# A second wait ahead of GpSimd's row gathers in a one-core graph-attention, mixing and expert kernel

## The reference

```python
xn = _layernorm(x)
h  = xn @ W_layer.T + b_layer
a1, a2 = h @ w_a1.T + b_a1, h @ w_a2.T + b_a2
v  = leaky_relu(a1[row] + a2[col], 0.01)
m  = segment_max(v, row)
att = exp(v - m[row]) / segment_sum(exp(v - m[row]), row)
x  = x + segment_sum(att[:, None] * h[col], row) + mix(xn)
x  = x + top2_of_8_experts(_layernorm(x))
```

## Time and profile before

| | before |
|---|---|
| time, median of 3 runs | 2761.94 us (2761.82 to 2765.81) |
| profiled execution, its span from first to last instruction | 2728.5 us |
| what lies around the span (median less span) | 33.4 us |
| mean granted TensorE clock | 0.853 |
| gathers issued | 878, from 355.2 to 1668.5 us |
| busy in the span: TensorE, VectorE, ScalarE, GpSimd | 84%, 66%, 47%, 42% |

### The profile page before, as it was taken

The page is one execution under the profiler, slowest core; times in us unless marked ns, Lnnn a source line. Parts: engine busy times, 40 slices in busy tenths (PEclk is TensorE's granted clock), DMA queues, the critical chain, the costliest instruction groups (busy, mean ns, idle before and its releaser), DMA issues.

```text
span 2728.5 us, 47082 instructions
## 1 busy us (share of the span) xinstructions
PE 2280.4 (84%) x12485; PEld 1867.1 (68%) x12485; DVE 1795.1 (66%) x6067; ACT 1281.0 (47%) x3812; POOL 1135.7 (42%) x1159
## 2 busy tenths in 40 slices
PE   4789948888888888888888877542999999999998
PEld 2566635666666666666666654432999999999997
DVE  8678747777777777777777777653555555555553
ACT  7666645555555555555555555541222222222222
POOL 0000046666666666666666663355122211222211
PEclk8899958887787788877878788555999999999999
DMA  2344324444444344444444335563222222222221
GB/s 81 96 131 137 102 80 107 111 112 114 112 111 113 106 112 113 113 112 115 107 109 114 108 97 56 191 196 127 35 36 36 35 36 36 34 36 36 34 36 28
DMA packets 148308, 245.62 MB, mean 90 GB/s; under 512 B 27873, under 2 KB 107618, under 8 KB 147286
## 3 DMA queue, kind: packets, MB, share of 16 engines
q0 software_dynamic: 62352, 142.72, 23.2%
q1 hardware_dynamic: 85702, 99.93, 12.1%
HBM read 182.39 MB, written 60.15 MB: 89 GB/s over the span
## 4 chain that ended last, share of the span: by engine, by line
PE 59%; issue 14%; DVE 12%; another core or an unknown queue 5%; DVEq 3%; ACT 3%; POOL 1%; DMA 1%; SPq 0%; ACTq 0%; POOLq 0%
PE psum L1703 19%; PE psum L1189 14%; PE psum L1736 10%; PE psum L1180 3%; PE psum L515 3%; DVE arena L1288 3%; DVEq L1307 2%; PE psum L1197 2%; PE psum L494 1%; PE psum L1471 1%; DVE arena L1299 1%; ACT arena L586 1%; DVE arena L1332 1%; DVE arena L1271 1%
## 5 line engine op out<-in xcount | busy, mean ns | idle before, releaser
L1140 POOL DMA_INDIRECT arena<-table,arena x878 | 849.8, 968 | 478.5 <-issue 233.4
L1189 PE MATMUL psum<-arena 128*128 128x257 f32 x1756 | 679.0, 509 | 196.6 <-DVE arena L1288 113.0
L1189 PEld LDWEIGHTS psum<-arena 128*128 128x128 f32 x1756 | 362.8, 240 | 410.7 <-issue 310.9
L1288 DVE SCALAR_TENSOR_TENSOR arena<-arena,psum 128x257 f32 x878 | 421.5, 480 | 295.1 <-remote 154.3
L1703 PE MATMUL psum<-arena 128*128 128x128 f32 x4620 | 550.6, 275 | 0.6 <-ACT arena L1758 0.6
L1703 PEld LDWEIGHTS psum<-arena 128*128 128x128 f32 x4620 | 541.0, 192 | 6.7 <-issue 0.9
L1840 POOL DMA_INDIRECT out<-arena x105 | 163.1, 1554 | 665.4 <-ACT arena L1765 615.7
L1216 ACT ACTIVATE arena<-arena 128x128 f32<-128x128 bf16 x880 | 281.1, 391 | 129.7 <-DVE arena L1302 74.9
L1180 PEld LDWEIGHTS psum<-arena 128*128 128x128 f32 x1760 | 272.3, 229 | 29.0 <-issue 23.0
L1736 PE MATMUL psum<-arena 128*128 x1260 | 290.5, 379 | 0.8 <-ACT arena L1765 0.8
L1229 ACT ACTIVATE arena<-arena 128x128 f32<-128x128 bf16 x880 | 281.2, 391 | 7.1
(11 more groups left out here) (338 smaller groups left out, 3010.3 us busy)
## 6 DMA issues: line engine op xcount, KB each, us to landing
mix_inputs<-arena SPq DMA_DIRECT2D x147, 128.0 KB
arena<-table,arena POOLq DMA_INDIRECT x878
arena<-expert_in SPq DMA_DIRECT2D x105, 129.0 KB
arena<-in_x SPq DMA_DIRECT2D x98, 128.0 KB
arena<-mix_inputs SPq DMA_DIRECT2D x49, 256.0 KB
arena<-in_w SPq DMA_DIRECT2D x6, 1364.0 KB
out<-arena SPq DMA_DIRECT2D x50, 128.0 KB
table<-arena SPq DMA_DIRECT2D x49, 129.0 KB
```

The costliest lines, as they stand in the source:

```text
L1140: pool.indirect_dma_start(rows_in[j][:, q * TW:(q + 1) * TW], None, table_d[:, :], bass.IndirectOffsetOnAxis(ap=col_all[:, t:t + 1], axis=0))\
L1189: mm(psum[4 + q][:, 0:C + 1], weight[b][:, q * P:(q + 1) * P], rows_in[g][:, q * TW:q * TW + C + 1], start=True, stop=True).then_inc(S("pr ...
L1288: v.scalar_tensor_tensor(here, here, alpha[(j - 5) % RING][:, q:q + 1], psum[4 + q][:, 0:C + 1], ALU.mult, ALU.add).then_inc(S("acc_done"), 1)
```

## The change

Before GpSimd issues the gathers of group i, from i = 2 on, it now also waits until `hot_ready` has reached i - 1, that is until VectorE has made the one-hots of group i - 2. The wait for the slot stays. Nothing else is different; lines behind it stand two further down (the gather is L1142).

```diff
                     if due((i - RING + 1) * G):
                         pool.wait_ge(S("product_done"), (i - RING + 1) * G)
+                    if due(i - 1):
+                        pool.wait_ge(S("hot_ready"), i - 1)
                     for q in range(REST if i == NG - 1 else G):
```

## The result

The changed kernel takes 2972.49 us (median of 4 runs, 2969.53 to 2982.17), the kernel before 2763.88 beside it (4 runs, 2761.82 to 2766.72): a ratio of 1.0752, interval 1.073 to 1.0774, or +208.6 us. The forecast was slower by 145.

A forecast was written before the change was run, and what follows sets the result against it. The gather stage was taken as bound by a cycle: eight gathers, then the time until TensorE's reports come through. +153 us for 212 groups less 8 at the start gave +145, so 2907 us; range 2620 to 3030.

The forecast's parts named there:

- its case: Gather stage: longer gather runs stall VectorE, 2907 us forecast, own range 2820 to 3050; given a chance of 0.55.
- the new wait is always the later one: GpSimd before each group's gathers: the one-hots wait ends after the slot wait, starting group 108's gathers 4.1 us later.
- the rows come in time: VectorE's reading of gathered rows: 3.6 us are left after wait and landing, so late rows cost nothing, 0 to 2 us.
- runs grow to twelve gathers: GpSimd's gather stream: three groups follow without a pause, then VectorE stops at its first addition, a step of 12.2 us.
- Two signs: Signs of being right in the gather stage: L1290 "remote" waits near 300 us and the last gather near 1810 us.
- A group at 6.7 us: Gather stage, groups 8 to 219: 6.7 us a group against 5.98, over 212 groups +153 us.
- The bound of 8.4 us: Far end for the gather stage: runs of two groups, VectorE stalled at the second's additions, 8.4 us a group, +510 us.
- GpSimd starting 0.3 us after the one-hots: GpSimd after VectorE's one-hots: gathers two groups ahead start 0.3 us later, the wait costed at nothing beyond that usual gap.
- Eight microseconds back at the start: Start of the gather stage: breaking up the run of 32 gathers saves 8 us, of between nothing and 18.6.
- The 33.4 us around the span: Outside the profiled span: 33.4 us added to the forecast span of 2873.5 us to give 2907.
- The reading of the cause: Gather stage: what TensorE reports late in a long run of gathers is seen only when the run has ended.
- broken runs, faster: Rival, gather stage: short pauses let TensorE's reports through, 5.4 us a group, 2631 us, best 2579; chance 0.33.

## Why the prediction was right, and where its sizes were off

**Direction and mechanism: right.** Slower, 2972.49 in the range of 2620 to 3030 and in the 2820 to 3050 of its case. The steps that held: the new wait is always the later one; the rows come in time; runs grow to twelve gathers, though in only 21 of 102; after such a run VectorE has stalled at its first addition, mostly for 7 to 8.6 us where 6 to 7 were forecast, and goes on 2.9 us after the last gather's start (median). The cycle above is the one that was worked out, with a stalled step of 11.46 us for 12.2. Two signs were off: "remote" waits of L1290 are 221.7 us for some 300, and the last gather is at 1905.5 us for 1810.

**A group at 6.7 us: too small.** It took 7.10. The forecast had VectorE get through the second step of each run, because "it uses reports from the first 5 us". Often it doesn't: the transposes' report is late too (182.6 us of "remote" waits at L1326 in 71 steps, where before had 9.8), and the run ends at eight. Half of all runs did. I had every run of twelve followed by one or two groups at 5.4 to 5.9 us, and these made the mean cheap. Runs of twelve took 7.5 us a group (7.25 forecast), but what lay between them was not cheap: runs of eight took 6.7 a group, and the few runs of four 9.7. The bound of 8.4 us, two groups that share a stall, was neared by some runs of eight (the longest took 16.2 us for two groups) and was not the rule.

**GpSimd starting 0.3 us after the one-hots: too small.** It was 0.75 or more (the L1304 of 1108.07 ended at 1108.75 and the gather came at 1109.51). The wait costed at nothing has a price of its own when GpSimd has nothing else to hide it, 0.46 us as measured later.

**Eight microseconds back at the start: too much.** Group 8 begins at 406.24 instead of 408.80.

**The 33.4 us around the span: wrong as a term.** The profiled execution of the changed kernel took 1.7 us more than its span (2973.84 against 2972.1). So the 33.4 were in the main the distance of one execution, which seems to have been quick, from the median. In spans the forecast was +145 and the result +243.6; in medians +145 and +208.6.

**The reading of the cause** ("seen only when the run has ended") was half right. That TensorE's reports are late is shown by the times of the raises, and in the kernel before they come through once a run has ended. In the changed kernel some come sooner: in 22 of the runs of eight VectorE's stall at L1326 ended before the last gather of the run was started. And four memsets between gathers, in runs of dozens, held nothing. What matters is how closely gathers follow each other. On these chips: runs of eight and twelve at 1.25 us hold reports; four at 1.25 and then a start 2.45 us later hardly do (5 of 778 raises late); a start 2.0 to 2.2 us later does, as much as before; 1.69 throughout doesn't. Why it happens, and why one chip of those used is free of it, stays open.

**The rule that was weighed.** The changed kernel's data came in time, and no engine's instructions got longer but the gathers named below; by that the rule of the Trainium skill, page "SBUF — State Buffer", section "SBUF: two separate sides", that a DMA isn't slowed by compute nor compute by DMA, isn't contradicted. But VectorE stood for up to 8.6 us at L1290 for work that TensorE had finished, while gathers were dense, so it can't be read to say that a dense stream of gathers leaves the other engines' timing alone.

The rival "broken runs, faster" was right that real breaks take the stalls away: with six memsets the changed kernel is back near the kernel before. It isn't faster than that, though: VectorE then waits for its rows. The wait alone makes no such breaks because gathers take 5.0 us and a short step 4.77.

## What to carry to other kernels

When two engines wait for a third whose work the timeline shows as long done, look at what stops just before both go on; here it was GpSimd's stream of indirect DMAs. Thinning it out or breaking it took the waits away, but each has its own price: four memsets a gather cost 6%, and nothing tried gained more than 0.6%. A wait that ties a producer to a consumer made no pauses here, as the consumer's short step (4.77 us) is no longer than the producer's burst (5.0); it only let the consumer's stall hold up the producer too. Before times from two chips are compared, compare the kernel before's: here 2497 and 2766 us came from the same program.

## What the runs showed that was not expected

**A gather that starts during VectorE's one-hots takes longer.** In the kernel before 68 of the 70 gathers over 1.1 us started while an L1302 was running, and those that started inside one had a mean of 1.15 us against 0.95 for the others (1.26 in the changed kernel, 1.35 with three memsets). Each of the long ones ended 0.81 to 0.83 us after that L1302 had, whenever it had started: the gather of 1102.09 above began with 0.57 us of the L1304 of 1101.97 to go and took 1.40. It waits for VectorE's instruction to end. With three memsets 148 gathers were long; that is most of the 0.35 us a group by which it missed GpSimd's own rate. The Trainium skill says on the page "SBUF — State Buffer", section "Who interferes with whom", that a VectorE instruction with two SBUF inputs contends with a GpSimd instruction that reads SBUF. L1302 has two such inputs and a gather reads its row numbers there; the numbers agree. How often the two meet depends on how the engines are in step: with two memsets a gather 9 gathers were long without the new wait and 162 with it.

**A second semaphore wait ahead of a gather isn't free.** 0.46 us a group where it stood between a memset and a gather, in the two traces above.

**Chips differ.** The kernel before took 2497.00 us on one chip and 2766 to 2767 on two others, each within 1%. Not all of the 269 us is the gather stage: from the last gather to the end it took 1060.0 us in the kernel before as profiled, and 1027.2 to 1031.2 in the four profiles of the quick chip. Its mean granted clock was higher too, 0.91 to 0.92 for the kernel before against 0.85 to 0.87; which of this is cause and which effect no run here shows.
